# A fill behind every fourth gather in place of a wait for a landing at every eighth

## The chip, the cores and the metric

The kernel runs on one core of a Trainium2 chip. Its time is the device time of one execution, in microseconds (us). Five engines work side by side, each on its own list of instructions: TensorE (PE in the profile), VectorE (DVE), ScalarE (ACT), GpSimd (POOL) and SyncE (SP). They wait for one another only by semaphores, counters that an instruction raises when it is done and that another engine's instruction waits for.

## What is computed

One layer of a graph network on 3125 nodes with 256 features, 53125 weighted edges (both directions and the self loops), followed by a mixture of experts. Cut to what matters here:

```python
xn = _layernorm(x)
msgs = edge_val[:, None] * xn[edge_col]                  # one row of 256 for each edge
h = segment_sum(msgs, edge_row, num_segments=3125) @ W.T + b
x = x + h + mix(xn)                                      # mix: linear attention, two projections with GELU, layer norms
x = x + ffn(_layernorm(x))                               # experts, weighted by a router
```

The part at issue is `xn[edge_col]` (a gather of rows) and the sum over edges.

## The kernel before

The nodes lie in 25 tiles of 128. The kernel first multiplies the normalized rows with W and writes them to memory as `xg_rows`. It sorts the edges on the chip by their target tile into 440 columns (`COLS`) of 128 slots. For each column GpSimd gathers the 128 source rows from `xg_rows` into a slot of a ring (`RING`, part of the tile that the profile calls ARENA); TensorE multiplies the gathered rows with a matrix that holds the edge weights at the place of their target (`SEL`, made by VectorE), which sums the edges of one target; VectorE adds the result to the tile of X that the column belongs to.

The ring has 18 slots (`RC`), three hands (`HANDS`) of six (`HAND`). Three waits bind the engines:

- `gather(c)`, lines 698 to 707: a slot is free when the pair of columns that lay in it 18 columns ago has been multiplied. GpSimd waits for that on line 704, at every even column, and issues the gather on line 705. Each hand has a semaphore, `gathered[hand]`, that every landing raises by 16.
- `pairs(lo, hi)`, TensorE, the matmuls of line 1799: two columns (a pair) go into one of two banks of results. At the first pair of a hand TensorE waits until all six columns of the hand have landed. At each pair it waits until VectorE has added the pair before the last, so that its bank is free. The second column's matmul raises `chunk_mm`.
- `add(base, c)`, VectorE, line 1289: it waits for `chunk_mm` of the pair and adds the bank to X. Selections (line 1277) for later columns stand between the additions.

The first 132 columns (`COLS_A`) are gathered while GpSimd still makes tables for sorting (`group_columns`, the products on line 693): six gathers, then a product, in turn, behind a first run of 14 gathers. The other 308 come in one loop at the end of GpSimd's list for this stage, lines 724 to 729:

```python
pool.wait_ge(slots_ready, 2)
for c in range(COLS_A, COLS):
    if (c - COLS_A) % BREATH == 0:
        pool.wait_ge(*landed(c - 1))
    gather(c)
```

`BREATH` is 8 (line 425) and `landed(c)` (line 514) names the semaphore and the count at which column c has landed. So GpSimd issues eight gathers, waits until the last of them has landed, and goes on. Nothing else stands on GpSimd's list between them.

TensorE's list is written out by hand: the pairs stand between the steps of other work. From 318 to 510 us loop A, the attention's keys and values: twelve steps of two tiles, each with the projections on line 1850 (and 1857), the outer products on line 1865, and 58 pairs spread over the twelve (`a_at`). From 510 to 790 us loop B: steps of two tiles with seven pairs each (`B_PAIRS`): attention (line 1895), a transpose of what ScalarE scaled (line 1636, XS), a hidden layer (line 1913, one group of its matmuls marks a step) and a projection (lines 1924 to 1927). Then come the experts, without gathers, on line 2008 and others. VectorE and ScalarE follow the same steps.

Of the kernel before, what the change touches and what calls it, by code (L numbers as in the profile page):

```python
# [5 lines left out]
def gps_layer_program(nc, x, row, col, weight, gnn_wT, gnn_b, qkv_wT, ln1_g, ln1_b, mix_w1T, mix_b1,  # L6
# [12 lines left out]
    P = 128  # L19
# [23 lines left out]
    HAND = 6  # L43
    HANDS = 3
    RC = HANDS * HAND
# [4 lines left out]
    COLS = EK + TILES - 1  # L50
# [20 lines left out]
    with ctx:  # L71
        def sb(name, shape, dt=f32):
            return scope.enter_context(nc.sbuf_tensor(name, shape, dt))

        def sem(name):
            return ctx.enter_context(nc.semaphore(name))
# [11 lines left out]
        ROWC = sb("ROWC", [P, 5, C])  # L88
        B2R, L2G, L2B, FG, FB = (ROWC[:, n, :] for n in range(5))
        carrier = sb("carrier", [P, 1])  # L90
        eps_ln = sb("eps_ln", [P, 1])
        warm = sb("warm", [P, 1])
        ident = sb("ident", [P, P])
# [232 lines left out]
        gathered = [sem(f"gathered{h}") for h in range(HANDS)]  # L326
# [95 lines left out]
        STEP_PAIRS = (PAIRS_A - PER) // LATER  # L422
        assert RC // 2 > PAIRS_A - STEP_PAIRS * LATER >= PER
        B_PAIRS = 7
        BREATH = 8
        B_FIRST = COLS // 2 - 12 - B_PAIRS * PAIRS

        def a_at(i):
# [81 lines left out]

        def pair_bank(pair):
            return bank[(2 if pair < PAIRS_A else 6) + pair % 2]

        def landed(c):

            r, at = divmod(c, RC)
            return gathered[at // HAND], 16 * (r * HAND + at % HAND + 1)

        def per_chunk(m, G, n):

# [92 lines left out]
        def _(pool):  # L613
# [84 lines left out]
            def gather(c):  # L698

                r, at = divmod(c, RC)  # L700
                k = at % HAND
                if r and k % 2 == 0:
                    pair = (c - RC) // 2
                    pool.wait_ge(chunk_mm[pair % 2], pair // 2 + 1)
                pool.indirect_dma_start(RING[:, at, :], None, xg_dram,  # L705
                                        bass.IndirectOffsetOnAxis(ap=SIX[:, c:c + 1], axis=0)
                                        ).then_inc(gathered[at // HAND], 16)
# [17 lines left out]
            pool.wait_ge(slots_ready, 2)  # L725
            for c in range(COLS_A, COLS):
                if (c - COLS_A) % BREATH == 0:
                    pool.wait_ge(*landed(c - 1))
                gather(c)


# [272 lines left out]
        def _(dve):  # L1004
# [260 lines left out]
            def targets(r, cols=RC):  # L1265

                _, base = nc.values_load_multi_w_load_instructions(
                    BID[0:1, bass.ds(r, 1), 0:cols].rearrange("p a c -> p (a c)"), engines=[mybir.EngineType.DVE],
                    min_val=0, max_val=(TILES - 1) * C,
                    skip_runtime_bounds_check_because="BID counts the buckets whose first column is at or before the "  # L1270
                    "column, less one: the first bucket starts at column 0, so it lies in 0 .. TILES - 1, times C")
                return base
# [235 lines left out]
            def over_sum(dst, width, n):  # L1508
# [14 lines left out]
            dve.wait_ge(topi_ready, 1)  # L1523
            dve.wait_ge(up_in, 16 * (NE + 1))
            _, chosen = nc.values_load_multi_w_load_instructions(
                RI[0:1, 0:TOPK], engines=[mybir.EngineType.DVE], min_val=0, max_val=NE - 1,
                skip_runtime_bounds_check_because="RI holds places of the NE experts that max_index found")
# [586 lines left out]
```

## Time and profile before

| | |
|---|---|
| time, median of 3 runs | 972.7 us (970.0 to 973.05) |
| the profiled execution | 975.65 us, of which its span is 973.9 |
| PE busy | 785.4 us (81%) |
| DVE busy | 677.2 us (70%) |
| ACT busy | 415.0 us (43%) |
| POOL busy | 584.6 us (60%) |
| granted clock of TensorE, mean | 0.925 |
| gathers (line 705) | 440, 426.6 us busy |

The span is the time from the first to the last instruction of one execution that the profiler recorded. Busy is the time in which an engine had an instruction at work. Idle time of an engine is put down to what ended it last: another engine's instruction, a DMA (a landing), "issue" where the engine waited for nothing that the profile shows, or "remote" where the releaser that the profile names had long been done.

### The profile page before, as it was taken

How to read it: one execution, taken by the hardware profiler on the slowest of the kernel's cores; microseconds unless marked ns; L12 is line 12 of the kernel's file. 1: busy time of each engine (PE TensorE's matmuls, PEld its weight loads, DVE VectorE, ACT ScalarE, POOL GpSimd, SP SyncE). 2: the span in 40 equal slices, each digit the busy share in tenths (PEclk: the TensorE clock that was granted, in tenths of full speed). 3: DMA queues.
4: the chain of work that ended last, by engine and by line, in shares of the span. 5: the costliest groups of instructions: out<-in, count | busy, mean ns of one | idle time of the engine just before them, and what ended most of it. 6: DMA issues, size and time to landing. Idle time of an engine off the chain costs nothing.

```text
span 973.9 us, 14063 instructions
## 1 busy us (share of the span) xinstructions
PE 785.4 (81%) x4353; PEld 639.0 (66%) x4353; DVE 677.2 (70%) x1936; ACT 415.0 (43%) x1008; POOL 584.6 (60%) x648
## 2 busy tenths in 40 slices
PE   7879857887787888878777877777776677999997
PEld 5649846776676566546545655565555454999997
DVE  8989737999875546445545767677667567766776
ACT  2738724775772133313313222332223216666551
POOL 3847675878877666666666666666666610333353
PEclk9989977999989799999988988989989889999999
DMA  7210032333233433333233333333332521000000
GB/s 238 87 49 1 28 92 60 93 88 88 87 91 92 111 87 103 87 87 108 82 105 90 114 87 84 106 91 108 90 111 87 100 30 55 13 22 24 23 29 30
DMA packets 38994, 76.88 MB, mean 79 GB/s; under 512 B 9811, under 2 KB 22536, under 8 KB 38920
## 3 DMA queue, kind: packets, MB, share of 16 engines
q0 software_dynamic: 21120, 57.70, 21.5%
q1 hardware_dynamic: 17800, 18.29, 5.9%
q8 instruction: 35, 0.57, 0.2%
q14 instruction: 39, 0.32, 0.1%
HBM read 69.48 MB, written 6.48 MB: 78 GB/s over the span
## 4 chain that ended last, share of the span: by engine, by line
PE 33%; issue 14%; POOL 11%; DVE 9%; ACT 4%; another core or an unknown queue 2%; DMA 1%; DVEq 1%; POOLq 0%; ACTq 0%
PE bank L2008 14%; POOL ARENA L705 11%; PE bank L1799 7%; DVE X L1289 4%; PE bank L1850 4%; ACT OIA L824 2%; PE bank L1857 2%; PE bank L1865 1%; PE bank L1636 1%; PE bank L1757 1%; PE bank L1913 1%; DMA ARENA<-xg_rows,ARENA 1%; DVE ARENA L1277 1%; DVE ST L1029 1%
## 5 line engine op out<-in xcount | busy, mean ns | idle before, releaser
L705 POOL DMA_INDIRECT ARENA<-xg_rows,ARENA x440 | 426.6, 970 | 214.5 <-issue 118.0
L1289 DVE TENSOR_TENSOR X<-bank,X 128x256 f32 x440 | 185.0, 420 | 217.0 <-PE bank L1799 91.2
L1799 PE MATMUL bank<-ARENA 128*128 128x256 f32 x880 | 246.7, 421 | 97.1 <-DVE X L1289 53.2
L1799 PEld LDWEIGHTS bank<-ARENA 128*128 128x128 f32 x880 | 173.1, 208 | 148.4 <-DVE X L1289 67.0
L1277 DVE TENSOR_SCALAR ARENA<-iota,ARENA 128x128 f32<-128x128 f32 x440 | 153.4, 354 | 0.0
L1757 PE MATMUL bank<-OIA,ASA 128*128 128x128 f32 x676 | 95.3, 308 | 14.8 <-DVE ASA L1207 5.8
L1757 PEld LDWEIGHTS bank<-OIA,ASA 128*128 128x128 f32 x676 | 93.7, 224 | 18.5 <-issue 17.4
L824 ACT ACTIVATE OIA<-iota,LANE 128x128 f32<-128x128 f32 x286 | 86.0, 388 | 13.9 <-PE bank L1757 13.6
L992 ACT ACTIVATE HF<-bank,FB 128x262 f32<-128x262 f32 (+1 forms) x96 | 46.8, 488 | 42.0 <-PE bank L2008 22.5
L868 ACT ACTIVATE NK<-bank 128x256 f32<-128x256 f32 x25 | 9.7, 388 | 123.0 <-PE bank L1850 101.7
L2008 PE MATMUL bank<-QH,W1L 128*128 128x262 f32 (+1 forms) x192 | 55.9, 291 | 2.3 <-DVE W1L L1535 1.7
L2008 PE MATMUL bank<-QH,W1H 128*128 128x262 f32 (+1 forms) x192 | 55.2, 287 | 0.0
L2008 PE MATMUL bank<-QL,W1H 128*128 128x262 f32 (+1 forms) x192 | 55.1, 287 | 0.0
L693 POOL TENSOR_TENSOR ASA<-LHA,EPC 128x832 f32<-128x832 f32 x26 | 41.3, 1590 | 22.6 <-DVE LHA L1192 20.8
L2008 PE MATMUL bank<-W2H,HFL 128*128 128x256 f32 x192 | 54.0, 281 | 0.0
L2008 PE MATMUL bank<-W2H,HFH 128*128 128x256 f32 x192 | 54.0, 281 | 0.0
L2008 PE MATMUL bank<-W2L,HFH 128*128 128x256 f32 x192 | 53.9, 281 | 0.0
L1850 PE MATMUL bank<-QKVW,XT 128*128 128x512 f32 x100 | 49.3, 639 | 0.0
L734 POOL TENSOR_TENSOR XN<-XN,B2C 128x256 f32<-128x256 f32 x25 | 18.8, 752 | 47.7 <-DVE B2C L1566 47.7
L992 ACT ACTIVATE HFH<-bank,FB 128x262 fp32r<-128x262 f32 (+1 forms) x96 | 47.0, 490 | 0.0
L833 ACT COPY GSW<-bank 64x128 f32<-64x128 f32 x32 | 8.3, 258 | 82.7 <-remote 32.4
L1574 DVE TENSOR_TENSOR HFL<-HF,HFH 128x262 fp32r<-128x262 f32 (+1 forms) x96 | 40.1, 467 | 4.2 <-ACT HFH L992 3.9
(317 smaller groups left out, 1532.6 us busy)
## 6 DMA issues: line engine op xcount, KB each, us to landing
ARENA<-xg_rows,ARENA POOLq DMA_INDIRECT x440
FW1A<-in_exp_w SPq DMA_DIRECT2D x8, 512.0 KB
xg_rows<-XGS SPq DMA_DIRECT2D x12, 256.0 KB, 2.1
out<-YO SPq DMA_DIRECT2D x24, 128.0 KB, 1.7
X<-in_x SPq DMA_DIRECT2D x1, 1664.0 KB, 12.7
X<-in_x SPq DMA_DIRECT2D x1, 1536.0 KB, 8.3
FW<-in_exp_w SPq DMA_DIRECT2D x2, 512.0 KB, 4.4
QKVW<-in_qkv_wT SPq DMA_DIRECT2D x1, 768.0 KB
```

Source lines behind the costliest of these rows:

```text
L693: made = pool.tensor_tensor(into[:, :, LC:2 * LC], lh, per_chunk(EPC, G, LC), ALU.mult)
L705: pool.indirect_dma_start(RING[:, at, :], None, xg_dram, bass.IndirectOffsetOnAxis(ap=SIX[:, c:c + 1], axis=0)).then_inc(gathered[at // HA ...
L824: ins = act.activation(into[:, k, :], iota[:, :], ACT.Abs, scale=-1.0, bias=LANE[:, G * GC + k:G * GC + k + 1])
L992: ins = act.activation(into, bank[s][:, 0:width], ACT.Gelu, bias=FB1[:, n // FJ, n % FJ:n % FJ + 1])
L1277: ins = V.tensor_scalar(SEL[:, t % 2 * HAND + k, :], iota[:, :], SLO[:, at], SW[:, at], ALU.is_equal, ALU.mult)
L1289: V.tensor_tensor(xt, pair_bank(pair)[:, half * C:(half + 1) * C], xt, ALU.add).then_inc(x_added, 1)
L1574: V.tensor_tensor(HFL[par][:, n, 0:width], HF[:, s, 0:width], HFH[par][:, n, 0:width].bitcast(f32), ALU.subtract).then_inc(hl_ready, 1)
L1757: ins = T.matmul(bank[s][:, 0:P], left[:, k, :], right[:, k, :], start=(k == 0), stop=(k == GC - 1))
L1799: ins = T.matmul(pair_bank(pair)[:, u * C:(u + 1) * C], SEL[:, t % 2 * HAND + k, :], RING[:, h * HAND + k, :], start=True, stop=True)
L1850: ins = T.matmul(bank[2 + s][:, :], XT[:, c, s, :], QKVW[:, c, C:3 * C], start=(c == 0), stop=(c == CC - 1))
L1857: ins = T.matmul(bank[5][:, h * 2 * P:h * 2 * P + n], QKVW[:, c, h * P:(h + 1) * P], XT[:, c, 0:len(slots), :], start=(c == 0), stop=(c == ...
L2008: ins = T.matmul(into, left, right, start=(m == 0), stop=(m == len(terms) - 1))
```

## The change

The wait for a landing goes, and with it `landed`. `BREATH` becomes 4, and at every fourth column of the tail loop, from column 132 on, GpSimd fills one element in each of the 128 partitions of a new tile `beat` with zero, ahead of the gather. Nothing reads `beat`. There were 39 waits; there are 77 fills. `gather` is as it was, its wait for a free slot included.

```diff
         carrier = sb("carrier", [P, 1])
+        beat = sb("beat", [P, COLS // 4])
...
-        BREATH = 8
+        BREATH = 4
...
-        def landed(c):
-
-            r, at = divmod(c, RC)
-            return gathered[at // HAND], 16 * (r * HAND + at % HAND + 1)
...
             for c in range(COLS_A, COLS):
                 if (c - COLS_A) % BREATH == 0:
-                    pool.wait_ge(*landed(c - 1))
+                    pool.memset(beat[:, c // 4:c // 4 + 1], 0.0)
                 gather(c)
```

## Rows read from the trace of the kernel before

**Rows 1.** The page's costliest groups: busy us, mean ns | idle before, what ended it.

```profile
L705 POOL DMA_INDIRECT ARENA<-xg_rows,ARENA x440 | 426.6, 970 | 214.5 <-issue 118.0
```

**Rows 2.** The chain of waits from 600 to 650 us, shares by line.

```profile
by line: POOL ARENA L705 61.4%; issue 39.3%; POOLq L704 0.1%
```

**Rows 3.** Timeline of GpSimd: start us, us, what [idle before <-what ended it].

```profile
612.05 0.95 POOL L705 DMA_INDIRECT ARENA<-xg_rows,ARENA  x1 [3.28 <-DMA ARENA<-xg_rows,ARENA]
...
620.82 0.95 POOL L705 DMA_INDIRECT ARENA<-xg_rows,ARENA  x1 [0.30 <-issue]
623.85 0.95 POOL L705 DMA_INDIRECT ARENA<-xg_rows,ARENA  x1 [2.09 <-DMA ARENA<-xg_rows,ARENA]
```

**Rows 4.** Waits of TensorE, 318 to 510 us: us in total, times, longest.

```profile
PE bank L1799 <- issue: 13.0, 7, 4.2
```

**Rows 5.** Waits of TensorE, 510 to 790 us.

```profile
PE bank L1799 <- issue: 20.7, 11, 5.3
```

**Rows 6.** Timeline of TensorE at the end of the gathers.

```profile
776.07 2.05 PE L1799 MATMUL bank<-ARENA 128*128 128x256 f32 x4 [5.34 <-issue]
...
787.61 2.90 PE L1799 MATMUL bank<-ARENA 128*128 128x256 f32 x6 [3.91 <-issue]
```

**Rows 7.** Timeline of TensorE: where four steps of loop A begin.

```profile
335.33 1.05 PE L1850 MATMUL bank<-QKVW,XT 128*128 128x512 f32 x1
...
350.10 0.59 PE L1850 MATMUL bank<-QKVW,XT 128*128 128x512 f32 x1
...
387.98 0.59 PE L1850 MATMUL bank<-QKVW,XT 128*128 128x512 f32 x1
...
510.37 0.59 PE L1850 MATMUL bank<-QKVW,XT 128*128 128x512 f32 x1
```

**Rows 8.** Timeline of TensorE: hidden layers of four steps of loop B.

```profile
528.73 0.80 PE L1913 MATMUL bank<-XT,W 128*128 128x256 f32 x1 [1.11 <-ACT XT L911]
...
546.81 0.38 PE L1913 MATMUL bank<-XT,W 128*128 128x256 f32 x1
...
611.35 0.48 PE L1913 MATMUL bank<-XT,W 128*128 128x256 f32 x1 [0.95 <-ACT XT L911]
...
777.90 0.42 PE L1913 MATMUL bank<-XT,W 128*128 128x128 f32 x1
```

**Rows 9.** Waits of TensorE, 534 to 613 us, the two largest.

```profile
PE bank L1636 <- ACT XS L900: 5.3, 2, 3.8
PE bank L1799 <- DVE X L1289: 4.6, 3, 2.5
```

**Rows 10.** Timeline of GpSimd: a fill; the first run, its product, the next gather.

```profile
3.67 0.13 POOL L625 MEMSET eps_ln<- 128x1 f32 x1
...
113.74 1.21 POOL L705 DMA_INDIRECT ARENA<-xg_rows,ARENA  x1 [4.27 <-DVE ARENA L1231]
...
130.30 0.95 POOL L705 DMA_INDIRECT ARENA<-xg_rows,ARENA  x1 [0.30 <-issue]
131.27 1.59 POOL L693 TENSOR_TENSOR ASA<-LHA,EPC 128x832 f32<-128x832 f32 x1
133.02 0.99 POOL L705 DMA_INDIRECT ARENA<-xg_rows,ARENA  x1 [0.16 <-issue]
```

**Rows 11.** Timelines of TensorE and VectorE: matmuls of pairs, and additions of them.

```profile
123.65 1.46 PE L1799 MATMUL bank<-ARENA 128*128 128x256 f32 x6
...
133.90 0.42 DVE L1289 TENSOR_TENSOR X<-bank,X 128x256 f32 x1 [6.37 <-remote]
...
619.15 1.13 PE L1799 MATMUL bank<-ARENA 128*128 128x256 f32 x4
...
623.70 0.42 DVE L1289 TENSOR_TENSOR X<-bank,X 128x256 f32 x1 [3.28 <-remote]
```

**Rows 12.** Waits of VectorE, 510 to 790 us.

```profile
DVE X L1289 <- remote: 28.9, 15, 4.3
```

**Rows 13.** The products of line 693: ns min/median/max, first and last start us.

```profile
L693 POOL TENSOR_TENSOR ASA<-LHA,EPC x26: 1582/1591/1603, 68.2 to 301.4; 128x832 f32<-128x832 f32 x26
```

## The prediction

> **What bounds the kernel now.** I read the page first, for the costly lines; then the chain of waits, to see which engine sets the pace in the stage that the change touches; then the timeline of that engine; then the waits of TensorE and VectorE over the same stage. The edit sits in the tail loop of GpSimd, columns 132 to 439, 308 of the 440 gathers. The page's row of line 705 has 970 ns for a gather and 214.5 us of idle time ahead of the gathers [rows 1]. In the middle of the stage the chain of waits is GpSimd alone: gathers 61.4%, and the "issue" between them 39.3% [rows 2]. The timeline shows what that is made of: eight gathers from 612.05 to 620.82 start (620.82 - 612.05) / 7 = 1.253 us apart, and the ninth, at 623.85, has 2.09 us of idle time ahead of it that a landing ended [rows 3]. So eight gathers take 623.85 - 612.05 = 11.80 us, where eight at 1.253 would take 10.02: one wait costs 1.78 us of GpSimd's time. There are 39 of them (columns 132, 140, ..., 436), 69 us on that engine.
>
> That is GpSimd's loss, not the kernel's. What the kernel loses is seen on the engine that uses the rows. TensorE multiplies a hand of six gathered columns, and asks for the landing of a whole hand ahead of its first matmul on line 1799. Ahead of that line it was idle for 13.0 us that the profile calls issue in loop A's stage [rows 4], and for 20.7 us in loop B's [rows 5]. These idle times stand ahead of the first matmul of a hand, and I read all of them as time in which TensorE was short of rows. That is the direct stake of the change, 33.7 us, and 9.2 of it lie at the end, where TensorE stood idle 5.34 us ahead of 776.07 and 3.91 ahead of 787.61 [rows 6].
>
> A second reading of the stake goes by the pace of the two loops, each with twelve steps here. Loop A went from 335.33 to 510.37, 14.59 us a step; three steps early in it, with the ring still nearly full, took 387.98 - 350.10 = 37.88, 12.63 a step [rows 7]. Loop B went from 528.73 to 777.90, 20.76 a step; its first took 18.08 (to 546.81), but the three behind that took 64.54, 21.5 a step [rows 8], and from 534 to 613 TensorE was not short of rows once: what it waited for longest there is ScalarE's XS, 5.3 us, with nothing on line 1799 from a landing or from issue [rows 9]. So A's own pace is well under what it ran at, by 12 x 1.96 = 23.5 us, while B's is not: if every step of B were like the first it would give 12 x 2.68 = 32.2, and if every step were like the next three, nothing. 55.7 is the most that the consumers could use.
>
> **The change part by part.** *Removed:* 39 waits for a landing, 1.78 us each. GpSimd still waits for a free slot at each even column (line 704), so it can't run over the ring; that wait now stands on the gather itself and is late next wherever the ring is full.
>
> *Added:* 77 fills of 128x1 f32 (columns 132, 136, ..., 436). None stands between gathers in the trace of before, so their price is bounded. A fill of this shape, at the kernel's start, has 0.13 us [rows 10]. The nearest row to one between gathers is the product of line 693: it starts 0.02 us after a gather's end (130.30 + 0.95 to 131.27), and the next gather starts 0.16 after its own [rows 10]. With 0.13 for a fill in its place that is 0.31 us from gather to gather, against 0.30 without it. The low end is a fill that lies wholly beside what follows, 0.02 + 0.16, a gain of 0.12; the high end is a full 0.30 on either side of 0.13, 0.43 more. I take 0.03, next to the product's row: 77 x 0.03 = 2 us in all, 1.26 a gather; the high end would be 33 us, 1.36 a gather. At 1.26 GpSimd needs 9.67 x 1.26 = 12.2 us for a step of loop A (116 columns in twelve steps) and 14 x 1.26 = 17.6 for one of loop B (seven pairs). Both are below the quick steps of [rows 7, 8], so the fills lie beside the consumers' work and cost nothing; GpSimd has 0.4 us a step to spare in A, and what it takes beyond that is paid.
>
> The Trainium skill has a rule on how to price the fill (Perfetto Trace Analysis, section GPSIMD Engine Instruction): a GpSimd span is unreliable, one goes by the spacing of starts. By that the 0.13 of [rows 10] is no price at all; any spacing that keeps GpSimd's step of A under 12.63 us leaves the sum as it is, and no row here shows a fill behind a gather.
>
> The vanished wait has a second side. TensorE's signals come late while gathers run back to back. The pair multiplied at 619.15 was done at 620.28; VectorE's addition of it started at 623.70, after 3.28 us of idle time that the profile puts down to "remote" [rows 11], and it started inside the wait for the landing, which lasted from 621.77 to 623.85. VectorE lost 28.9 us in 15 such waits in loop B's stage [rows 12]. So the wait that is removed is also a pause in which these signals come through. In the only run of 14 gathers without a pause (113.74 to the product at 131.27, [rows 10]) they came later still: matmuls done at 125.11, the addition at 133.90, 6.37 us of it idle [rows 11]. The change makes such runs the rule, unless a fill is pause enough. No row shows that: the pauses in which signals came have 1.77 us (the product's) or 2.09 (the wait's) without a gather, and a fill leaves about 0.3.
>
> Two things speak for a mild outcome all the same. A signal that is held back also stops GpSimd (it waits for the same matmuls at line 704 once the 18 slots are full), so a pause comes of itself. And a fill is a computing instruction of GpSimd, as the product is that ended the long run.
>
> **Sum.** In A the 13.0 us of shortage go, in full, since its own pace has room for more (23.5). At the end the 9.2 go. Of B's other 11.5 us I take half, 5.8, because its unhurried steps were no quicker than the short ones. The fills cost nothing. 13.0 + 9.2 + 5.8 = 28.0. The profiled execution took 975.65 us (span 973.9 and 1.75 around it): 947.65. The median of the runs is 2.95 below it: 944.7, in round numbers 945.
>
> **The rivals.** *Hidden.* B's pace belongs to the chain between VectorE, ScalarE and TensorE, and rows that come sooner only wait. For it speak [rows 9]. Then A's gain is all, and part of it is handed back at the seam between the loops: 958 to 972.
>
> *More than the shortage.* The fill is pause enough, TensorE's signals are on time, and both loops go at their quick steps: 972.7 - 55.7 = 917, up to 925 with B at 18.8. For it: signals were late only well into a run, and a fill comes every four gathers.
>
> *The fill is dear*, 0.43 us, or held behind the gather ahead of it. GpSimd at 1.36 needs 13.2 us a step in A and 19.0 in B, which takes up to 7 us of A's gain and some of B's: 945 to 960.
> [...]
>
> *Slower: TensorE's signals are starved.* The mechanism is that of [rows 11], at every hand-over from TensorE to VectorE and to GpSimd. A fill is no pause; a run ends when the ring is full, and only then do the signals come. Price: between two releases go the pairs whose signals are on time early in a run, about two, and the two that fill the banks, four pairs or eight gathers; GpSimd issues those in 10.0 us and stops for 2 to 3 us, as in [rows 3]: 1.50 to 1.63 us a gather, where it is 1.475 over [rows 3]. Over 308 that is +8 to +48; with three pairs, six gathers in 7.5 + 2.5 us, 1.67 and +59. It decides from where the signals' further delay exceeds the 28 us that the waits give, 0.7 us for each of the 39. 976 to 1030, most likely near 990.
>
> *The change does not do what it says*: pauses stay where the waits went, because GpSimd is blocked at line 704 as often as it was by landings. That is the mild form of the rival before, and gives no change.
>
> **How the numbers follow.** The forecast, shortage gone and signals no later than now, has 0.37, with a range of its own from 925 to 958 (all of [rows 7]'s 23.5 and more of B's at one end, half of the 28 at the other). More than the shortage: 0.12. Dear fill: 0.08. Hidden: 0.13, half of it within 0.3% of no change (2.9 us, about what a measurement of this kernel can tell). Starved: 0.30, of which 0.03 is near no change. Faster: 0.37 + 0.12 + 0.08 + 0.06 = 0.63; the same 0.07 + 0.03 = 0.10; slower 0.27. The range leaves out the worst of the starved cases, about 0.10 above 1000, and what beats the quick steps, below 914.
>
> **What would show it.** Right: no row of line 705 with a landing as releaser; gathers 1.25 to 1.30 apart over a fill; idle time ahead of line 1799 down from 33.7 us towards 6; steps near 13 in A and 20 in B; a full ring (line 705 idle until the matmuls of line 1799) in place of landings. Wrong by price: starts more than 1.4 apart over a fill. Wrong by mechanism: VectorE's "remote" idle time in B's stage above 28.9 us, single waits beyond 4 us, and GpSimd blocked for a slot whose matmul is long done. Hidden: the shortage gone, and B still at 21.

## The result

The changed kernel takes 1007.15 us (median of 4 runs, 1003.43 to 1008.92) where the kernel before took 972.88 beside it: a ratio of 1.0349, with an interval of 1.0321 to 1.0377. It is 34 us slower. The prediction had 945 us, a range up to 1000, and 0.27 for slower: wrong in sign, and 7 us beyond its range. The rival that came true is the one called starved signals. Two runs stand far above their fellows, one of e4 (2546 us) and one of the kernel before beside e5 to e8 (1486 us), and no ratio below counts them.

The profiled execution of the changed kernel took 1003.43 us, the quickest of the four, with a span of 1001.7, 27.8 us more than before. Lines below 515 have moved up by four: 705 is now 701, 1289 is 1285, 1799 is 1795, 1850 is 1846, 1913 is 1909, and the fill is line 724.

First the fills, in GpSimd's timeline (start us, us, what, idle time before and what ended it). Those below answer to [rows 3]:

```profile
323.65 0.95 POOL L701 DMA_INDIRECT ARENA<-xg_rows,ARENA  x1 [0.30 <-issue]
324.59 0.12 POOL L724 MEMSET beat<- 128x1 f32 x1
324.90 0.94 POOL L701 DMA_INDIRECT ARENA<-xg_rows,ARENA  x1 [0.19 <-issue]
```

A gather starts 1.25 us after the one before it, with a fill between them as without. Where a slot is free the fill costs nothing, and no gather waits for a landing any more. Next, what GpSimd waited for from 318 to 830 us (total, times, longest):

```profile
POOL ARENA L701 <- PE bank L1795: 71.4, 26, 7.5
POOL ARENA L701 <- issue: 71.2, 245, 0.6
POOL ARENA L701 <- remote: 40.2, 23, 3.0
```

Before, the landings had cost GpSimd 76.4 us of idle time in this stage, and slots that were not free 12.2. Now the slots cost 71.4 + 40.2 = 111.6. The removed waits have come back at line 700, larger. What TensorE waited for ahead of the pairs, from 318 to 510 us and from 510 to 815, in answer to [rows 4, 5]:

```profile
PE bank L1795 <- issue: 1.4, 2, 1.1
...
PE bank L1795 <- issue: 2.2, 3, 1.7
```

The shortage of rows is gone, 33.7 us down to 3.6, as forecast. And yet both loops are slower. Where their steps begin, in answer to [rows 7, 8]:

```profile
335.04 0.70 PE L1846 MATMUL bank<-QKVW,XT 128*128 128x512 f32 x1 [1.51 <-issue]
...
515.33 0.59 PE L1846 MATMUL bank<-QKVW,XT 128*128 128x512 f32 x1
...
540.91 0.80 PE L1909 MATMUL bank<-XT,W 128*128 128x256 f32 x1 [1.11 <-ACT XT L907]
...
811.90 0.38 PE L1909 MATMUL bank<-XT,W 128*128 128x128 f32 x1
```

| stage | before, us | after, us | |
|---|---|---|---|
| up to loop A's first step | 335.3 | 335.0 | -0.3 |
| loop A, twelve steps | 175.0 | 180.3 | +5.3 |
| between the loops | 18.4 | 25.6 | +7.2 |
| loop B, twelve steps | 249.2 | 271.0 | +21.8 |
| from there to the end | 196.0 | 189.8 | -6.2 |
| span | 973.9 | 1001.7 | +27.8 |

Part of this is not idle time. TensorE's granted clock stands at one of two levels, 2.4 or 1.2 GHz; its mean went from 0.95 of the upper one to 0.91 in loop A and from 0.90 to 0.84 in loop B. Loop B before and after (the window and its length, then the busy us of PE, PEld, DVE, ACT and POOL with their instructions, the granted clock, the DMA share, GB/s):

```profile
528.73:777.90 249.17, 185.28 (x798) 143.00 (x799) 171.41 (x635) 72.35 (x119) 158.54 (x167) 0.90 0.36 98
```

```profile
540.91:811.90 270.99, 201.64 (x799) 153.94 (x799) 171.25 (x635) 71.13 (x119) 156.72 (x199) 0.84 0.34 88
```

The same matmuls keep TensorE busy for 16.4 us longer in loop B, and for 5.0 in loop A (148.3 us, 143.3 before): most of the 21.8 and 5.3 us that the loops lost. TensorE's idle time grew by 0.3 us in loop A and by 5.5 in loop B: the shortage of rows went, and waits of another kind came. What the clock did behind such waits is seen from 639 us on: TensorE had stood still for 5.41 us ahead of 639.48, the granted clock was 1.00 from 643.2 to 660.0 and 0.50 from 660.2 to 673.6.

Those other waits, and how a step of loop B goes now, are seen from 624 to 647 us, on GpSimd, TensorE, VectorE and ScalarE:

```profile
624.38 0.95 POOL L701 DMA_INDIRECT ARENA<-xg_rows,ARENA  x1 [4.93 <-PE bank L1795]
...
635.64 0.94 POOL L701 DMA_INDIRECT ARENA<-xg_rows,ARENA  x1 [0.31 <-issue]
636.58 0.12 POOL L724 MEMSET beat<- 128x1 f32 x1
638.89 0.94 POOL L701 DMA_INDIRECT ARENA<-xg_rows,ARENA  x1 [2.19 <-remote]
...
646.82 0.95 POOL L701 DMA_INDIRECT ARENA<-xg_rows,ARENA  x1 [3.12 <-PE bank L1795]
```

```profile
630.46 1.89 PE L1909 MATMUL bank<-XT,W 128*128 128x256 f32 x8
632.18 1.89 PE L1795 MATMUL bank<-ARENA 128*128 128x256 f32 x8
639.48 2.07 PE L1920 MATMUL bank<-W,HS 128*128 128x256 f32 x4 [5.41 <-ACT HS L912]
```

```profile
638.75 0.42 DVE L1285 TENSOR_TENSOR X<-bank,X 128x256 f32 x1 [4.03 <-remote]
```

```profile
638.59 0.84 ACT L912 ACTIVATE HS<-bank,B1C 128x256 f32<-128x256 f32 x2 [7.34 <-remote]
```

GpSimd issues ten gathers without a pause (624.38 to 636.58), two fills among them and one behind them. TensorE has the hidden layer done at 632.35 and two pairs at 634.07. ScalarE, which waits for the hidden layer, starts on it at 638.59, and VectorE on the pairs at 638.75: both some 2 us after GpSimd's last gather ended, though what they waited for had been done for 4.7 to 6.2 us. GpSimd itself had stopped because the slot it wanted was held by a pair whose signal was late as well. TensorE, which needs ScalarE's result, stands still for 5.41 us. Fourteen gathers take 22.4 us, 1.60 each. VectorE lost 38.6 us to such waits from 510 to 790 us, in answer to [rows 12], and 62.8 from 318 to 830:

```profile
DVE X L1285 <- remote: 38.6, 13, 4.5
...
DVE X L1285 <- remote: 62.8, 22, 7.9
```

and TensorE, from 510 to 790 us, this to ScalarE's hidden layer:

```profile
PE bank L1920 <- ACT HS L912: 36.9, 9, 5.4
```

From 318 to 840 us the remote waits are VectorE's, ScalarE's and GpSimd's. TensorE has none, before or after: what VectorE and ScalarE signal to it comes on time.

### The profile page after: what moved, and what is told of

Its sections match the earlier page's. It is cut to its first block, busy times and chain, and to the rows that moved or that the text cites. A ratio compares the mean times of both kernels' runs of the same rounds, so it can differ in the third digit from the quotient of the medians.

```text
span 1001.7 us, 14101 instructions
## 1 busy us (share of the span) xinstructions
PE 804.7 (80%) x4353; PEld 652.4 (65%) x4353; DVE 676.6 (68%) x1936; ACT 415.0 (41%) x1008; POOL 596.2 (60%) x725
## 4 chain that ended last, share of the span: by engine, by line
PE 37%; DVE 15%; another core or an unknown queue 8%; issue 8%; ACT 4%; DVEq 1%; POOLq 0%; POOL 0%; ACTq 0%
PE bank L2004 13%; PE bank L1795 8%; DVE X L1285 6%; PE bank L1846 4%; PE bank L1920 2%; PE bank L1853 2%; DVE ARENA L1273 2%; PE bank L1861 2%; PE bank L1632 1%; PE bank L1923 1%; PE bank L1753 1%; PE bank L1922 1%; DVE ST L1025 1%; ACT L912 1%
## 5 line engine op out<-in xcount | busy, mean ns | idle before, releaser
L1795 PE MATMUL bank<-ARENA 128*128 128x256 f32 x880 | 241.2, 415 | 56.3 <-DVE X L1285 49.4
L1273 DVE TENSOR_SCALAR ARENA<-iota,ARENA 128x128 f32<-128x128 f32 x440 | 151.0, 348 | 0.0
L1753 PE MATMUL bank<-OIA,ASA 128*128 128x128 f32 x676 | 93.1, 304 | 15.5 <-DVE ASA L1203 5.8
L1753 PEld LDWEIGHTS bank<-OIA,ASA 128*128 128x128 f32 x676 | 91.6, 220 | 19.5 <-issue 18.4
L1920 PE MATMUL bank<-W,HS 128*128 128x256 f32 x100 | 42.2, 565 | 42.6 <-ACT HS L912 41.9
L1920 PEld LDWEIGHTS bank<-W,HS 128*128 128x128 f32 x100 | 24.1, 265 | 57.1 <-ACT HS L912 45.9
L689 POOL TENSOR_TENSOR ASA<-LHA,EPC 128x832 f32<-128x832 f32 x26 | 41.3, 1589 | 21.3 <-DVE LHA L1188 18.3
L1846 PE MATMUL bank<-QKVW,XT 128*128 128x512 f32 x100 | 46.5, 608 | 1.5 <-issue 1.5
## 6 DMA issues: line engine op xcount, KB each, us to landing
X<-in_x SPq DMA_DIRECT2D x1, 1664.0 KB, 12.2
```

Source lines behind the costliest of these rows:

```text
L689: made = pool.tensor_tensor(into[:, :, LC:2 * LC], lh, per_chunk(EPC, G, LC), ALU.mult)
L1273: ins = V.tensor_scalar(SEL[:, t % 2 * HAND + k, :], iota[:, :], SLO[:, at], SW[:, at], ALU.is_equal, ALU.mult)
L1753: ins = T.matmul(bank[s][:, 0:P], left[:, k, :], right[:, k, :], start=(k == 0), stop=(k == GC - 1))
L1795: ins = T.matmul(pair_bank(pair)[:, u * C:(u + 1) * C], SEL[:, t % 2 * HAND + k, :], RING[:, h * HAND + k, :], start=True, stop=True)
L1846: ins = T.matmul(bank[2 + s][:, :], XT[:, c, s, :], QKVW[:, c, C:3 * C], start=(c == 0), stop=(c == CC - 1))
L1920: T.matmul(bank[3 + s][:, 0:C], HS[:, h, s, :], W2[:, h, :], start=(h == 0), stop=False)
```

## The experiments

Two theories stood against each other at first. *Starved signals:* TensorE's signals are held back while GpSimd issues gathers, and the removed waits were the pauses in which they came through. *Something else of the change:* the fills do harm, or it was the landing that counted, few transfers in flight. The edits of e4, e7 and e8 are shown against the kernel before, all others against the changed one. Each ratio is to runs of the kernel before on the same chip, with its interval.

| kernel | us | ratio | VectorE's remote waits, 318 to 840, us |
|---|---|---|---|
| before | 972.7 | 1 | 37.5 |
| after | 1007.15 | 1.0349 (1.0321 to 1.0377) | 62.8 |
| e1, neither wait nor fill | 1014.99 | 1.0416 (1.0385 to 1.0447) | 60.0 |
| e2, both | 976.2 | 1.0014 (0.9994 to 1.0035) | 32.3 |
| e3, six chained fills at every 8th | 986.27 | 1.0114 (1.0083 to 1.0145) | 76.8 |
| e5, eight chained fills at every 8th | 973.4 | 0.9976 (0.9947 to 1.0006) | 22.5 |
| e4, plain loads by SyncE | 898.74 | 0.9211 (0.9173 to 0.9248) | none |
| e7, landing wait at every 16th | 1002.74 | 1.0252 (1.0176 to 1.0328) | 78.2 |
| e8, landing wait at every 4th | 1042.98 | 1.0697 (1.0634 to 1.076) | none |
| e6, two chained fills at each gather | 999.52 | 1.0235 (1.0172 to 1.0298) | none |
| e9, one fill at each gather | 1013.58 | 1.041 (1.0384 to 1.0437) | 65.7 |
| e10, two chained fills at every 2nd | 968.98 | 0.9973 (0.994 to 1.0005) | 68.6 |
| e11, two chained fills at every 4th | 978.14 | 1.005 (1.0023 to 1.0077) | 82.1 |
| e12, two small chained fills at each | 978.14 | 1.0046 (1.0025 to 1.0066) | 69.2 |
| e13, half rows, neither wait nor fill | 1017.44 | 1.0404 (1.0362 to 1.0446) | 64.2 |
| e14, two middle-sized fills at each | 975.29 | 0.9989 (0.9965 to 1.0012) | 45.7 |
| e15, four chained fills at every 4th | 973.08 | 0.9959 (0.9932 to 0.9987) | 38.5 |
| e16, e10 up to loop B, then e12 | 983.83 | 1.0104 (1.0067 to 1.014) | 73.9 |

**The two halves of the change.** e1 takes the waits out and puts nothing in:

```diff
-                if (c - COLS_A) % BREATH == 0:
-                    pool.memset(beat[:, c // 4:c // 4 + 1], 0.0)
                 gather(c)
```

> The waits are taken out and no fill is put in. Starved signals (TensorE's signals come through only in a pause of about 1.8 us without a gather, and a fill is none): the same as the changed kernel, 1000 to 1015 us, with runs of ten gathers and more and VectorE's remote waits above 55 us from 318 us on. The fills do the harm (they cost GpSimd or VectorE something): about the forecast of the first prediction, 940 to 955. The fills let some signals through: slower than the changed kernel, 1020 or more.

e2 keeps the wait at every eighth gather and puts the fills in beside it:

```diff
-        BREATH = 4
+        BREATH = 8
...
                 if (c - COLS_A) % BREATH == 0:
+                    pool.wait_ge(*landed(c - 1))
+                if (c - COLS_A) % 4 == 0:
                     pool.memset(beat[:, c // 4:c // 4 + 1], 0.0)
```

> The wait at every eighth gather stays, and the 77 fills are put in beside it. Starved signals: the fills are free and do nothing, 970 to 977 us, as before. The fills do the harm: 990 or more, most of the way to 1007. The fills let signals through: below 968.

e1 took 1014.99 us and e2 976.2. The whole loss lies in the removal. The fills alone do nothing that can be measured (1.0014); in place of the waits they leave the kernel about 8 us below e1, a small part of what the waits were worth, and with four times as many fills e9 below is back at e1's time, so a gain from them is not shown. That they harm is out.

**Is it GpSimd's gathers?** e4 lets SyncE load the tail's rows with plain transfers, in order instead of by the edges, behind the same waits for slots; GpSimd's loop is empty. TensorE waits on semaphores of their own (`loaded`) for these columns.

```diff
+            for c in range(COLS_A, COLS):
...
+                sp.dma_start(RING[:, at, :], xg_dram[bass.ds(c % (TILES - 1) * P, P), :]).then_inc(loaded[at // HAND], 16)
...
-            for c in range(COLS_A, COLS):
-                if (c - COLS_A) % BREATH == 0:
-                    pool.wait_ge(*landed(c - 1))
-                gather(c)
```

> The 308 rows of the tail come by plain loads that SyncE issues, with the same waits for a free slot and as many bytes, and GpSimd issues nothing there; the rows are taken in order, not by the edges, so the sums over edges are left wrong. Starved signals by GpSimd's issuing of gathers: no TensorE signal late from 320 us on, VectorE's remote waits there under 5 us, and both loops near their own pace: 12.6 us a step in A, 17 to 19 in B, 905 to 940 us. The traffic into the ring holds the signals back, not the issuing: remote waits stay at 35 us or more, and the time at 965 or more.

It took 898.74 us, better than the expectation's own lower end. What VectorE waited for from 318 to 840 us, largest first:

```profile
DVE X L1297 <- PE bank L1810: 82.1, 41, 7.7
DVE X L1297 <- issue: 16.2, 15, 1.8
```

No "remote" row is left; the loops took 154.2 and 199.0 us (175.0 and 249.2 before):

```profile
333.30 0.59 PE L1861 MATMUL bank<-QKVW,XT 128*128 128x512 f32 x1
...
487.46 0.59 PE L1861 MATMUL bank<-QKVW,XT 128*128 128x512 f32 x1
...
506.21 0.80 PE L1924 MATMUL bank<-XT,W 128*128 128x256 f32 x1 [1.11 <-ACT XT L919]
...
705.17 0.63 PE L1924 MATMUL bank<-XT,W 128*128 128x128 f32 x2
```

So without gathers B goes at 16.6 us a step, and the kernel before already paid some 75 us to its gathers: shortage, late signals and the lower clock together. In loop B the granted clock is 0.98 in e4 (0.90 before) and TensorE is busy for 169.5 us (185.3 before), so that 15.7 of the 50.2 us gained there are matmuls that ran faster; no run changes the clock alone. e4 changes who issues, how rows are looked up and how they travel. e13 was to part these: e1 with half of each row, 512 bytes in place of 1024, as many rows and gathers (it takes them from other places, and leaves out the right sums over edges).

```diff
-            def gather(c):
+            def gather(c, width=C):
...
-                pool.indirect_dma_start(RING[:, at, :], None, xg_dram,
+                pool.indirect_dma_start(RING[:, at, 0:width], None, xg_dram.rearrange("n (a c) -> (n a) c", c=width),
...
-                gather(c)
+                gather(c, C // 2)
```

> The kernel with neither wait nor fill; each gather of the tail takes 128 rows of half the width, 512 bytes in place of 1024 (from other places, so the sums over edges are left wrong); as many rows and instructions, half the bytes. The issuing holds the signals: as with whole rows, remote waits of VectorE from 318 us on at 50 us or more, 1000 to 1018 us. The bytes hold them: remote waits below 30 us, 960 or less.

1017.44 us, and VectorE's waits as in e1. GpSimd's queue on the page, e1 first (packets, MB, share of 16 engines):

```profile
q0 software_dynamic: 21120, 57.70, 21.0%
```

```profile
q0 software_dynamic: 16192, 37.51, 14.6%
```

A third of the queue's bytes less, and a quarter of its packets, changes nothing. So it is GpSimd's gathers that hold the signals back, and not their bytes. Whether it is the issuing itself, or the 128 row look-ups that each gather sets going, e4 and e13 do not part: e4 takes both away and e13 keeps both.

**Is it the pause, whatever fills it?** e3 has six fills of 128x110 at every eighth gather, each waiting for the one before; e5 has eight.

```diff
+        paused = sem("paused")
...
-        BREATH = 4
+        BREATH = 8
...
-                    pool.memset(beat[:, c // 4:c // 4 + 1], 0.0)
+                    for k in range(6):
+                        paused_at = (c - COLS_A) // BREATH * 6 + k
+                        if paused_at:
+                            pool.wait_ge(paused, paused_at)
+                        pool.memset(beat[:, 0:110], 0.0).then_inc(paused, 1)
```

> No wait for a landing; at every eighth gather six fills of 128x110, each waiting for the one before it, so that GpSimd issues no gather for an estimated 1.5 to 2.2 us (a fill of 128x128 had 0.21 us in the trace before; the hand-over between two is not known). Starved signals: the pause is what counts, whatever GpSimd does in it: 965 to 982 us, VectorE's remote waits from 318 us on near the 37.5 us of before. The landing counts (few transfers in flight): as the changed kernel, 1000 or more.

> As the kernel with six fills, with eight, so that GpSimd's time without a gather, 1.60 us there, becomes about 2.1, that of the landing waits of before. Starved signals, the length of the pause counts: 970 to 979 us. The landing counts, or a busy GpSimd does not let signals through as an idle one does: 984 or more, as with six fills.

The chains on GpSimd's timeline, e3 and then e5:

```profile
403.79 1.45 POOL L729 MEMSET beat<- 128x110 f32 x6
405.39 0.95 POOL L702 DMA_INDIRECT ARENA<-xg_rows,ARENA  x1 [0.15 <-issue]
```

```profile
600.15 1.94 POOL L729 MEMSET beat<- 128x110 f32 x8
602.25 0.95 POOL L702 DMA_INDIRECT ARENA<-xg_rows,ARENA  x1 [0.15 <-issue]
```

With 1.60 us without a gather the kernel took 986.27, with 2.10 us 973.4, as with the landing waits. e3 missed what either theory had for it, 965 to 982 or 1000 and more: I had taken 1.5 us to be enough. e5 came as the theory of the pause had it. No landing is waited for in either; e5 shows that a busy GpSimd lets the signals through as well as a waiting one, so long as it issues no gather. These two do not rule out the landing, though: a wait for one took 2.09 us behind the gather's end [rows 3], and the signals of the step shown above came 2.0 us behind it. So rows were still on their way at the end of e3's pause, and few or none at the end of e5's. The landing falls with e6 below.

**How often?** e7 and e8 are the kernel before with `BREATH` 16 and 4.

> The wait for a landing at every sixteenth gather in place of every eighth. Starved signals: half the pauses, between before and the kernel with neither: 985 to 1008 us, and GpSimd blocked for free slots where the waits went. Runs of 16 as good as runs of 8, and only their absence hurts: 970 or less.

> The wait for a landing at every fourth gather. Starved signals: nearly none is late any more (VectorE's remote waits from 318 us on below 10 us), but GpSimd takes (4 x 1.253 + 1.78) / 4 = 1.70 us a gather, 308 x 1.70 = 523 us for the tail, where it took 469: 1015 to 1035 us, bound by GpSimd, TensorE short of rows. If lateness were not tied to the length of a run, remote waits would stay near 37 us.

Half the pauses lose 27 us (1002.74, where before took 975.64 beside it). Twice the pauses leave no remote wait, and cost more than those did: 1042.98, 8 us above the expected range, with TensorE short of rows instead,

```profile
PE bank L1799 <- issue: 91.3, 32, 6.1
```

in e8, against the 33.7 us of [rows 4, 5]. The tuned eight is a bargain between the two.

**Long pauses or short gaps?** e6 puts two chained fills of 128x110 behind every gather (the code of e3 with 2 in place of 6, `BREATH` 1).

> No landing waits; behind every gather two fills of 128x110, the second waiting for the first, so that gathers start about 1.48 us apart (0.53 without a gather each time), the mean pace of before, evenly. Signals need one long pause: starved as in the changed kernel, 1000 to 1020 us, VectorE's remote waits above 55 us. Signals need a share of time without gathers, however it is cut: on time, and 940 to 970 us.

I had estimated 1.48 us a gather; it became 1.565:

```profile
600.83 0.45 POOL L729 MEMSET beat<- 128x110 f32 x2
601.44 0.95 POOL L702 DMA_INDIRECT ARENA<-xg_rows,ARENA  x1 [0.15 <-issue]
602.38 0.46 POOL L729 MEMSET beat<- 128x110 f32 x2
602.99 0.95 POOL L702 DMA_INDIRECT ARENA<-xg_rows,ARENA  x1 [0.15 <-issue]
```

No wait of VectorE for its additions is "remote" any more, so no pause of 2 us is needed: 0.61 us at each gather does as well. Nor do rows have to be at rest. TensorE, short of rows, began a hand 1.87 us behind the end of the hand's last gather (598.32 + 0.95), when the next had long been issued (599.87):

```profile
598.32 0.95 POOL L702 DMA_INDIRECT ARENA<-xg_rows,ARENA  x1 [0.15 <-issue]
...
599.87 0.95 POOL L702 DMA_INDIRECT ARENA<-xg_rows,ARENA  x1 [0.15 <-issue]
...
601.14 3.32 PE L1800 MATMUL bank<-ARENA 128*128 128x256 f32 x7 [2.60 <-issue]
```

So at this pace some rows are always on their way, and the signals come on time. The time of 999.52 is that of the expectation's first case, or just under it; its cause is not: GpSimd has become the bound, and TensorE stood idle 68.3 us ahead of the pairs. Then the same pair of fills at every second gather (e10), at every fourth (e11, the place of the change's own fill), and smaller ones: one fill of 128x1 at each (e9), two chained ones of 128x1 at each (e12).

> No landing waits; one fill of 128x1 behind every gather, so that the fills alternate with the gathers but the gathers stay about 1.25 us apart. The gap is what counts: starved, 1000 to 1018 us, VectorE's remote waits from 318 us on above 50 us. An instruction of another kind between two gathers is what counts, one for each: signals on time, GpSimd no longer the bound, 900 to 935 us.

> No landing waits; behind every second gather two fills of 128x110, the second waiting for the first: gaps of 0.30 and 0.61 us in turn, (1.253 + 1.565) / 2 = 1.41 us a gather, 434 us for the tail where the spread kernel took 482. Signals drain in gaps of 0.6 us, every second one is enough: remote waits below 10 us and 940 to 962 us. Only a gap at every gather is enough: remote waits above 30 us and 975 or more.

> The same pair of fills at every fourth gather, the place of the changed kernel's fill, with a gap of 0.61 us in place of its 0.31: 1.33 us a gather, 410 us for the tail. If a gap of 0.6 us is enough there: remote waits below 15 us and 915 to 945 us. If not: near the changed kernel, 990 to 1010.

> Two fills of 128x1 behind every gather, the second waiting for the first: gaps between 0.30 and 0.61 us, estimated 0.45 (the spread kernel's pair took 0.45 with 110 elements each, and a fill of one has 0.12 where one of 110 has 0.19), 1.40 us a gather. Gaps of that size drain the signals: remote waits below 10 us and 935 to 960. They don't: 985 or more.

e9 and e11 belong together. A fill at each gather, 308 in all, that leaves the gathers 1.25 us apart does nothing (1013.58, e1's time). Two fills at every fourth gather that leave 0.61 us there are worth 29 us against the changed kernel (978.14). It is not the instruction between the gathers but the time without one. Beyond that my expectations of these failed: all three times of e10 to e12 lie between their two cases. The signals are still late (68.6 to 82.1 us), and yet the times are 37 to 46 us below e1's. VectorE's remote waits are no measure of the loss by themselves: VectorE can sit through a late signal without TensorE standing still. What TensorE stood still for is ScalarE's hidden layer; from 318 to 840 us, in e1 and in e10:

```profile
PE bank L1918 <- ACT HS L910: 42.3, 10, 5.5
```

```profile
PE bank L1925 <- ACT HS L917: 7.0, 3, 3.2
```

That wait is long in the slow kernels (41.9 us in the changed one, 39.0 in e9, 39.5 in e13, 22.2 in e7) and short in e11 (11.3) and e12 (none). It is not all of the loss either: e3 has 4.4 us of it and takes 986.27.

Two more at the pace of the kernel before, one with even gaps of 0.50 us (e14: two fills of 128x50 at each gather), one with 1.1 us at every fourth (e15: four fills of 128x110):

> Two fills of 128x50 behind every gather, the second waiting for the first: estimated gap 0.50 us (0.61 with 110 elements, 0.42 with one), 1.45 us a gather, 447 us for the tail. If 0.5 us is enough, as 0.61 was: remote waits below 10 us, GpSimd the bound, 960 to 970 us. If not: remote waits above 30 us and 972 to 985.

> Four fills of 128x110 in a chain at every fourth gather: a gap of about 1.1 us there, 1.253 + 0.8 / 4 = 1.45 us a gather. Twice the gap of the pair at every fourth gather, so fewer signals are late: 962 to 974 us, remote waits between 15 and 60. If only pauses of 2 us or gaps at each gather drain them, 978 or more.

975.29 and 973.08: as the kernel before, or 0.4% below it. At an even 0.50 us there are remote waits again (45.7 us), at 0.61 there were none.

e10 and e12 had each shown one loop quicker than before in its profile: A in 166.1 us (e10), B in 244.3 (e12). e16 joins them.

> No landing waits; two chained fills of 128x110 at every second gather up to the columns of loop A's last step, two chained fills of 128x1 behind every gather from there on. If the stages' times add: 974 - 8.9 in A - 4.9 in B = 960 us. If loop B's gain was the scatter of one profiled execution, or the two are not independent: 966 to 978, no difference from before that matters.

It took 983.83, worse than either. Loop A, with e10's code, took 180.3 us this time, and no run shows why: a stage's time in one profiled execution can't be added to another's. Of the kernels that compute the whole only e15 has an interval below 1, by 0.1 to 0.7%; as the best of several that lie close to 1 it is not shown to be faster.

## Why the prediction was wrong

*The removed waits and the shortage: right.* No landing is waited for, and the idle time ahead of line 1799 went from 33.7 us to 3.6, a little further than the 6 that was forecast.

*The price of the fill: right.* 0.31 us from gather to gather was forecast; it is 0.30 to 0.31 (324.60 to 324.90 lies in the gap that was there). The rule of the Trainium skill on spans (Perfetto Trace Analysis, section GPSIMD Engine Instruction) held: the fill's span is 0.12 us and its price by the spacing of starts nothing. The dear fill did not come: the 77 fills took 112 to 227 ns, with a median of 118, and 55 of the gathers behind them started 0.30 to 0.31 us after the end of the gather ahead, as without a fill.

*The step that failed* is the condition on the sum, "signals no later than now". The prediction had seen the mechanism, its rows [rows 11, 12] and the long first run, and priced it; it then gave it 0.30 for two reasons, and both were wrong. The first was that a held-back signal stops GpSimd, so that a pause comes of itself. It does, but at the worst moment: it comes when the ring is full and VectorE, ScalarE and TensorE have stood still already, 4 to 7 us each (638.59, 638.75, 639.48). A wait at every eighth gather pauses before that. The second was that a fill is an instruction like the product that ended the first long run. e9 and e11 show that an instruction in the gap is not what counts; by that the product did it by its 1.77 us without a gather. So the 28.0 us of the sum went unpaid although the shortage went: waits for late signals, and a lower clock, took more.

*The rival's price* was of the right kind. It had four pairs or eight gathers to a release, 1.50 to 1.63 us a gather; loop B ran at 271.0 / 12 / 14 = 1.61 and loop A at 180.3 / 116 = 1.55. It left out who else waits for TensorE: ScalarE's hidden layer came 6.2 us late in the step shown, and TensorE waited 36.9 us for it from 510 to 790 us. It left out the clock too, and with it the 16.4 us by which TensorE's busy time grew in loop B. With 990 as its likeliest and a tenth cut off above 1000, the range ended 7 us short.

*The end of the gathers* can't be read from the table. Behind loop B's last step the changed kernel takes 6.2 us less, but of the forecast's 9.2 only the 3.91 ahead of 787.61 lay there, and 3.2 of the 6.2 are TensorE's busy time (173.9 us, 177.0 before).

*The stake was mis-sized.* I took 55.7 us for the most that the consumers could use, from quick steps of the loops themselves. e4 gave some 75. B's quick step of 18.1 us was its first, and that one takes 18.3 in e4 too (506.21 to 524.50); the eleven behind it take 16.4 there, quicker than any of before. The forecast "hidden" rival, that B's pace was its own, rested on steps without a shortage [rows 9]; by e4 those 21.5 us were no pace of B's chain, and with no shortage in them the late signals and the lower clock are what remains.

What stays open: why an even gap of 0.61 us at each gather ends the lateness and one of 0.50 does not, what in a gather holds TensorE's signals back, and how much of the loss the clock would make by itself. The e6 kernel was bound by GpSimd, as e8 was, so that the pairs came at another pace there too.

## What to carry to other kernels

Before a wait is taken out as too long, ask what else goes on while the engine stands still: here the wait cost 1.78 us a time and gave other engines' signals the time to come through. Idle time that the profile puts down to a releaser that was done long before is worth a look at what the other engines were doing when it ended; if it mostly ends in the same kind of pause, that pause is part of the kernel. And a loss of time in a stage is worth splitting into idle and busy time: here most of it was TensorE at a lower clock. A full ring that stops the producer is no substitute for a short pause ahead of it, since by then the consumers have stopped too.

## What the runs showed of the hardware

While GpSimd issues indirect gathers 1.25 us apart, TensorE's signals reach the other engines late, by 6.2 us in the step shown; with the rows loaded by SyncE, VectorE has no remote wait (898.74 us). Half the bytes in a gather change nothing (1017.44 against 1014.99). A pause of 2.1 us at every eighth gather keeps the loss down whether GpSimd waits (972.7) or fills (973.4) in it; one of 1.60 does less (986.27); with 0.61 us at every gather VectorE has no remote wait, in a kernel that GpSimd has come to bound (999.52), and an instruction in a gap that stays at 0.30 does nothing (1013.58). With late signals TensorE's granted clock fell, from 0.90 to 0.84 in loop B, and without gathers it was 0.98 there.
